# Selective scan in a ViT tower: seven of 32 B rows reach GpSimd by broadcast transfer of fp32 rows

## The reference, cut to what matters

```python
sel = jnp.einsum('ble,se->bls', xc, sel_w)
dt_in = sel[..., :R_]
Bm = sel[..., R_:R_ + N_]
Cm = sel[..., R_ + N_:]
dt = jax.nn.softplus(jnp.einsum('blr,er->ble', dt_in, dt_w) + dt_b)
dA = jnp.exp(dt[..., None] * A)
dBu = dt[..., None] * Bm[:, :, None, :] * xc[..., None]
def step(h, inp):
    dA_t, dBu_t, C_t = inp
    h = dA_t * h + dBu_t
    y = jnp.einsum('ben,bn->be', h, C_t)
    return (h, y)
```

## Time and profile before

| | before |
|---|---|
| median of 3 runs | 1512.79 us |
| lowest, highest | 1504.69, 1515.6 us |
| the profiled execution | 1513.76 us, span 1512.0 us |
| PE busy | 1292.1 us (85%) |
| DVE busy | 1031.3 us (68%) |
| ACT busy | 592.0 us (39%) |
| POOL busy | 455.7 us (30%) |
| mean granted clock of PE | 0.943 of full |

### The profile page before, as it was taken

How to read it: one execution, slowest core, us unless ns; L and a number is a source line. 1 busy time by engine, 2 the same in 40 slices (tenths; PEclk the granted TensorE clock), 3 DMA queues, 4 the chain that set the end, 5 groups by cost and what they waited for, 6 DMA issues and landing times. The chain is left out here.

```text
span 1512.0 us, 16650 instructions
## 1 busy us (share of the span) xinstructions
PE 1292.1 (85%) x5930; PEld 562.1 (37%) x5930; DVE 1031.3 (68%) x1130; ACT 592.0 (39%) x815; POOL 455.7 (30%) x230
## 2 busy tenths in 40 slices
PE   6957789989995778998998677999899677899988
PEld 2222333348532223333742223333473232333366
DVE  3599965664449996567555999556756599865683
ACT  0354343333425344332525443532451634343245
POOL 3268800022005881001200788000210189600030
PEclk9979999997897999999999799999999889999998
DMA  8334420000003342000001344200000134220000
GB/s 245 104 129 155 146 69 12 1 1 1 15 0 129 143 143 83 22 1 1 2 15 44 113 149 143 69 2 1 1 1 15 59 125 167 98 57 0 1 2 15
DMA packets 43379, 93.66 MB, mean 62 GB/s; under 512 B 6786, under 2 KB 23970, under 8 KB 42786
## 3 DMA queue, kind: packets, MB, share of 16 engines
q1 hardware_dynamic: 42690, 88.25, 17.5%
q10 hardware_dynamic: 608, 4.34, 1.0%
HBM read 87.84 MB, written 4.73 MB: 61 GB/s over the span
## 5 line engine op out<-in xcount | busy, mean ns | idle before, releaser
L448 POOL TENSOR_TENSOR scratch<-scratch 128x1024 f32<-128x1024 f32 x124 | 297.4, 2413 | 354.7 <-DVE scratch L1152 353.1
L598 PE MATMUL ps<-scratch,consts 128*128 128x512 f32 x512 | 257.8, 638 | 6.2 <-POOL scratch L448 6.2
L462 POOL TENSOR_TENSOR scratch<-scratch,rmax 128x1024 f32<-128x1024 f32 x32 | 61.6, 1925 | 598.3 <-DVE rmax L1272 598.3
L1152 DVE TENSOR_TENSOR_SCAN scratch<-ps,scratch 128x1024 f32<-128x1024 f32 x100 | 225.5, 2278 | 0.5
L925 ACT ACTIVATE ps<-steps,vec 128x1024 f32<-128x1024 f32 x128 | 142.9, 1117 | 207.1 <-DVE scratch L1152 205.2
L1201 DVE TENSOR_TENSOR scratch<-scratch,ps 128x1024 f32<-128x1024 f32 x108 | 131.8, 1221 | 128.6 <-PE ps L659 117.7
L576 PE MATMUL ps<-bc,pick 128*128 128x512 bf16 x256 | 84.7, 416 | 139.0 <-DVE scratch L1141 101.7
L971 ACT ACTIVATE scratch<-ps 128x1024 f32<-128x1024 f32 x108 | 108.9, 1023 | 175.5 <-PE ps L646 175.5
L598 PEld LDWEIGHTS ps<-scratch,consts 128*128 128x128 f32 x512 | 104.8, 207 | 127.2 <-issue 100.5
L646 PE MATMUL ps<-h_odd,w 64*128 64x512 f32 x512 | 140.9, 636 | 3.8 <-ACT scratch L971 3.8
L1141 DVE TENSOR_TENSOR scratch<-steps,ps 128x1024 f32<-128x1024 f32 x100 | 122.0, 1220 | 28.8 <-PE ps L576 23.5
(11 more groups left out here) (197 smaller groups left out, 1610.0 us busy)
## 6 DMA issues: line engine op xcount, KB each, us to landing
scratch<-c_rows SPq DMA_DIRECT2D x128, 512.0 KB, 3.7
steps<-routed_table SPq DMA_DIRECT2D x128, 64.5 KB, 1.9
decayT<-in_decayT SPq DMA_DIRECT2D x8, 512.0 KB, 15.6
work<-in_table ACTq DMA_DIRECT2D x1, 2064.0 KB, 13.2
routed_table<-work SPq DMA_DIRECT2D x1, 2064.0 KB, 6.3
w<-in_w ACTq DMA_DIRECT2D x4, 512.0 KB, 20.8
out<-h_even SPq DMA_DIRECT2D x4, 512.0 KB, 2.6
bc<-in_x_next SPq DMA_DIRECT2D x3, 512.0 KB, 3.6
```

The lines of the kernel that those rows point to most:

```text
L448: pool.tensor_tensor(hc_slot(k), hs_slot(k), c_slot(k), ALU.mult).then_inc(sem["hc_ready"], 1)
L598: m = mm(ps[:, 6 + c, :], ident, hc_slot(k)[:, c * CH:(c + 1) * CH], start=(n == 0), stop=(n == NS - 1))
L1152: dve.tensor_tensor_scan(hs_slot(k), banks(dA_bank(k)), dbu_slot(k), 0.0, ALU.mult, ALU.add).then_inc(sem["scanned"], 1)
```

## The change

For the seven POOL units B[n] no longer goes through PE and ACT. The store to DRAM now takes all 32 rows (B and C) of each batch instead of the 16 C rows, from the same fp32 tiles; SP loads row B[n] with a broadcast into `b_sb`, like a C row. SP's new transfer for unit j stands in front of the C load of unit j-1 and waits for the scan of the POOL unit before (j-4). POOL's multiply for j stands behind hc of unit j-3, one place later than before, and waits for the transfer. PE spreads B for the 25 DVE units only, in their own order, and ACT's copies are gone.

```diff
-B_ORDER = list(range(2 * NS))
-for _j in POOL_DRIVES:
-    B_ORDER[_j - 1:_j + 1] = [_j, _j - 1]
+DVE_DRIVES = [k for k in range(2 * NS) if k not in POOL_DRIVES]
@@ block.sync, move
-                sp.dma_start(c_dram[0], c_rows(0)[NS:2 * NS]).then_inc(sem["c_stored"], 16)
+                sp.dma_start(c_dram[0], c_rows(0)).then_inc(sem["c_stored"], 16)
...
-                        sp.dma_start(c_dram[1], c_rows(1)[NS:2 * NS]).then_inc(sem["c_stored"], 16)
+                        sp.dma_start(c_dram[1], c_rows(1)).then_inc(sem["c_stored"], 16)
                     if k == NS:
                         sp.wait_ge(sem["c_stored"], at(pair, "c_stored", 32))
+                    if k + 1 in POOL_DRIVES:
+
+                        n_ = POOL_DRIVES.index(k + 1)
+                        if n_:
+                            sp.wait_ge(sem["scanned"], at(pair, "scanned", POOL_DRIVES[n_ - 1] + 1))
+                        g_, row = divmod(k + 1, NS)
+                        sp.dma_start(b_sb, c_dram[g_, row].partition_broadcast(P)).then_inc(sem["b_loaded"], 16)
                     if k >= C_RING:
                         sp.wait_ge(sem["hc_ready"], at(pair, "hc_ready", k - C_RING + 1))
-                    sp.dma_start(c_slot(k), c_dram[g, n].partition_broadcast(P))\
+                    sp.dma_start(c_slot(k), c_dram[g, NS + n].partition_broadcast(P))\
@@ block.gpsimd
-                    if k + 4 in POOL_DRIVES:
-                        j = k + 4
+                    if k + 3 in POOL_DRIVES:
+                        j = k + 3
...
-                        pool.wait_ge(sem["b_copied"], at(pair, "b_copied", n_))
+                        pool.wait_ge(sem["b_loaded"], at(pair, "b_loaded", 16 * n_))
@@ block.tensor, spread_b and the loop that calls it
-                    k = B_ORDER[i]
+
+                    k = DVE_DRIVES[i]
...
                     if i:
-                        last = B_ORDER[i - 1]
-                        if last in POOL_DRIVES:
-                            pe.wait_ge(sem["b_copied"], at(pair, "b_copied", POOL_DRIVES.index(last) + 1))
-                        else:
-                            pe.wait_ge(sem["dbu_ready"], at(pair, "dbu_ready", drives_up_to(last)))
+                        pe.wait_ge(sem["dbu_ready"], at(pair, "dbu_ready", i))
...
-                    if k + 2 in POOL_DRIVES:
-                        spread_b(k + 1)
-                        spread_b(k + 2)
-                    elif k and k + 1 < 2 * NS and k + 1 not in POOL_DRIVES:
-                        spread_b(k + 1)
+                    if k in DVE_DRIVES[1:-1]:
+                        spread_b(DVE_DRIVES.index(k) + 1)
@@ block.scalar
-                def copy_b(j):
-                    act.wait_ge(sem["b_ps"], at(pair, "b_ps", B_ORDER.index(j) + 1))
...
-                    act.activation(b_sb, banks(0), ACT.Copy).then_inc(sem["b_copied"], 1)
...
-                    if k + 2 in POOL_DRIVES:
-                        copy_b(k + 2)
@@ block.vector, drive
-                    dve.wait_ge(sem["b_ps"], at(pair, "b_ps", B_ORDER.index(k) + 1))
+                    dve.wait_ge(sem["b_ps"], at(pair, "b_ps", drives_up_to(k)))
```

More of the change, by code:

```diff
@@ L70 @@
     dt_read=2, dt_exp=2, dt_ln=2, dt_ready=1, dt_late=NN, mid_late=1, u_ready=1, u_late=NN,
-    b_ps=2 * NS, dA_ready=2 * NS, dbu_ready=2 * NS - len(POOL_DRIVES), b_copied=len(POOL_DRIVES),
+    b_ps=2 * NS - len(POOL_DRIVES), dA_ready=2 * NS, dbu_ready=2 * NS - len(POOL_DRIVES), b_loaded=16 * len(POOL_DRIVES),
     dbu_pool=len(POOL_DRIVES), scanned=2 * NS, hc_ready=2 * NS - 1, hc_last=NC,
@@ L145, in build_tower @@
         fiT = sb("fiT", [P, 2, HID])
-        c_dram = nc.dram_tensor("c_rows", (2, NS, T), F32, kind="Internal").ap()
+        c_dram = nc.dram_tensor("bc_rows", (2, 2 * NS, T), F32, kind="Internal").ap()
         table_dram = nc.dram_tensor("routed_table", (P, LAYERS, NX, WCOL), F32, kind="Internal").ap()
@@ L926, in decay @@
                        .then_inc(sem["dA_ready"], 1)
-                def copy_b(j):
-                    act.wait_ge(sem["b_ps"], at(pair, "b_ps", B_ORDER.index(j) + 1))
-                    n_ = POOL_DRIVES.index(j)
-                    if n_:
-                        act.wait_ge(sem["scanned"], at(pair, "scanned", POOL_DRIVES[n_ - 1] + 1))
-                    else:
-                        act.wait_ge(sem["c_stored"], at(pair, "c_stored", 16))
-                    act.activation(b_sb, banks(0), ACT.Copy).then_inc(sem["b_copied"], 1)
                 first_parts(0)
```

## The result

| | before | after |
|---|---|---|
| median of 20 runs | 1520.07 us | 1497.95 us |
| lowest, highest | 1504.68, 1727.38 us | 1488.3, 1518.05 us |
| the profiled execution's span | 1512.0 us | 1493.3 us |
| four stretches of scans, added | 459.28 us | 444.19 us |

The ratio is 0.9883 with an interval of 0.9848 to 0.9917: 1.17% faster, where 0.78% was forecast. In pair 1 of the kernel before these are the two DVE rows

A forecast was written before the change was run, and what follows sets the result against it. DVE sets the pace in the scans, POOL next. Removed waits of 4.26 us a pair (17.0 in all), less 1.3 for held pieces, leave 2.94, or 11.8 in four pairs: 1512.79 to 1501.0 us, range 1488 to 1516.

The forecast's parts named there:

- the prediction's own signs: Expected in the trace: spread waits about 5 us, four units 12.75, stated piece lengths, no POOL wait for B.
- Spreads and copies removed: PE and ACT: busy time buys nothing; DVE's shorter waits for spreads give 4.26 us a pair, 17.0 in all.
- POOL's drive one place later: POOL's drive starts after hc j-3, ending at 8.3 for scan j at about 10.45; costs nothing by itself.
- The 2.1 us of slack: Time POOL's drive has in hand before scan j needs it, said to cover the later place.
- The pieces: DVE's small two-tile instructions, held by running POOL multiplies: 1.3 us given back of 4.26 a pair.
- The walk: Step through DVE's eight pieces in a pair against POOL's multiplies, ending 2.94 us ahead.
- The mis-sized term: DVE's piece L1178 after scan 24, held by hc 23: 1.98 us, not 1.40, so 0.58 lost a pair.
- rival A: Pieces after scans 4, 7, 8 and 24 not held by POOL: 1487.6 us, with half of it 1495; chance 0.18.
- the 4.5 of the sum: B load's assumed landing in us, between middle 3.7 and worst 6.0 of the C loads.
- Rival B: More pieces held, or PE's sums become the wait, 2 to 4 us a pair back: say 1511 us; chance 0.17.
- Rival C: B load lands late, past 8.0 us, delaying POOL's drive: 1549 us at 10; chance 0.09 with its second way.
- the second way of rival C: Fewer spreads halve PE's clock in a pair's last sums and projections: 36 us, 1537; chance 0.09 with late load.

The follow-up runs named there:

- e8: Changed kernel with the seven spreads that follow a POOL unit made twice, without the chain: scans 448.97 us, ratio 0.9894 to the kernel before.
- e3: Kernel before with only POOL's drive moved behind hc of unit j-3, spreads and copies kept: scans 456.13 us, ratio 0.9913.
- e7: Changed kernel with SP sending B's load one scan later, after scan j-3: scans 459.65 us, ratio 1.0071 to the kernel before.
- e2: Changed kernel without B's loads, POOL multiplying by tile xc instead (wrong output): scans 447.48 us, ratio 0.9816 to the kernel before.
- e6: Changed kernel with POOL's drive put back behind hc of unit j-4, transfer kept: scans 486.23 us, ratio 1.0156 to the kernel before.
- e5: Changed kernel with DVE's pieces at other scans, two bc pieces made one, gating behind the last products: scans 429.71 us, ratio 0.9823.
- e4: Changed kernel with only the tables changed, moving DVE's pieces to other scans: scans 436.31 us, ratio 0.9721 to the kernel before.
- e1: Changed kernel with PE spreading all 32 rows and ACT copying seven into an unread tile again: scans 456.01 us, ratio 1.0013.
- e9: e5 with B's load in front of the C load of unit j-2 instead of j-1: scans 425.68 us, ratio 0.9767 to the kernel before.

## Why the prediction was right

Forecast 1501.0 us, 0.78% under the median of before; measured 1.17% (0.83 to 1.52), so the mechanism and the side were right and the size somewhat low. In the profile: 11.8 us forecast from the scans, 15.1 and 12.6 measured in two profiles. What the first has over the forecast comes by luck from one piece, as told below. By the prediction's own signs two things did not come as said: POOL was not to wait for B, and waited 12 times, and the piece after scan 24 had another length.

- **Spreads and copies removed.** Right. The waits for the spread fell to 5.8 us where about 5 was said, and the busy time on PE and ACT bought nothing (e8).
- **POOL's drive one place later.** Right in the sum: the piece after scan 6 fell to 0.40, 2.05 us a pair, of which the pieces after scans 7 and 8 take some 1.4 back (e3: 1.57 and 0.93 instead of 0.69 and 0.40); what is left, about 0.7 a pair, is most of what the place alone gives (e3, 3.2 us in four pairs). The 2.1 us of slack were there for DVE: POOL waits up to 1.3 us for B without a scan waiting for POOL. e7, later by a whole scan, is past it.
- **The pieces.** The walk gave about 1.7 to 1.9, 0.40, 1.7 to 1.9 for the first three and measured were 1.71, 0.40 and 1.72; the fourth, which it had end 0.37 ahead, took 0.93 and ended 0.58 ahead, counted from the first scan. In pair 2, where the gating piece took 1.99 as forecast, the stretch is 2.78 us shorter than before, with 2.94 forecast. The trace agrees with the Trainium skill ("SBUF — State Buffer", the section on the two physically separate sides) that whoever starts first keeps the other out, on both sides: the piece is held (1.99), or hc is (pair 1).
- **The mis-sized term: the gating after scan 24.** I gave it 1.98 in each pair, 0.58 lost. Measured were 0.67, 1.99, 1.04 and 0.67, so that instead of 2.3 us lost 1.2 were won: these 3.5 us are the whole of the 3.3 by which the forecast was too small. In the second profile (7.2 in sum) 1.6 were lost, and the scans came within 0.8 us of the forecast. Behind this term stands the sentence that POOL should not wait for the loads. I had B's load go out at the end of scan j-4, since the C load in front of it on the queue waited for an older hc. For unit 25 that is hc 20, and it was not yet done: scan 21 ended at 159.68, but hc 20 was the second of three from 155.91 and ended near 160.6, and the queue shows B's issue just behind it (SP), 1.3 us late:

```profile
158.29 2.63 SPq L371 DMA_DIRECT2D scratch<-bc_rows  x2
160.98 0.42 SPq L368 DMA_DIRECT2D work<-bc_rows  x1
```

  This load landed after 5.36 us, at 166.3, and POOL's drive started 0.86 us late, as much as the lead that the walk gives POOL at this place: 9.14 - 8.3 = 0.84, not the "0.9 us or more" that the text on rival A says. In the four pairs the load of unit 25 went out 1.3, 1.1, 1.5 and 1.9 us after scan 21 and landed 5.4, 5.0, 5.7 and 4.9 us later. The landing was in the range of 4 to 6, though over the 4.5 of the sum; alone it would have made POOL wait at this unit in no pair, since B was wanted at 5.95. An engine's lag behind the scans, which I had not put into the queue's wait, came on top. e2, without the load, is the kernel of my walk, and has 1.96 or 1.97 in every pair.
- **Rival A, the pieces get in freely:** false for the three early pieces, true for the gating piece in two pairs of the first profile and in none of the second (0.90 at the least), and by the cause that the rival names, B's landing. **Rival B, the gain is used up:** false, two drives wait for 0.5 us and no further piece was caught. (Its price was added up wrongly: 2 to 4 us in each of four pairs give 1509 to 1517, not 1505 to 1515.) **Rival C, the load comes late:** false here, but its mechanism is real and near: one scan later (e7) or one place earlier (e6) brings it, and e6 costs 42 us more than the change in the scans. PE's clock was 1.00 in the last 10 us of the pair's scans, so the second way of rival C did not come either.

## What to carry to other kernels

When an engine sets the pace without waiting for anything, look for instructions of one shape with two lengths: here the same piece takes 0.40 or 2.45 us, and moving the pieces to scans for which the other engine itself waits, or into a wait, gave about as much in the scans (444 to 430 us, e5) as the change itself. Work such a table out again from the trace after each change, because removed waits shift which places are free (e4). And a transfer that shares a queue goes when the one in front of it may go: before counting its landing time, work out what that one waits for, with the lag of the engine that releases it.

## What was unexpected of the hardware

**PE at half clock while fully busy.** The stretch between two pairs' scans lasts 253 to 259 us, but in some pairs of several kernels 267 to 269: in the kernel before once, in e1 twice, in e3, e7 and e9 once (and in e9 once more behind the last pair), in the changed kernel not in its two profiles. It is a place in the attention block; here pair 1 of the kernel before (columns as in the earlier trace rows; the clock is the third number from the end):

```profile
340.00:350.00 10.00, 10.00 (x62) 7.54 (x62) 5.29 (x11) 2.25 (x3) 1.90 (x1) 0.50 0.01 2
350.00:360.00 10.00, 10.00 (x63) 8.54 (x62) 5.31 (x8) 3.09 (x4) 2.05 (x2) 0.52 0.00 0
```

and pair 2 of the same execution, at the same place of the program:

```profile
720.00:730.00 10.00, 10.00 (x114) 8.15 (x114) 8.82 (x17) 5.05 (x7) 4.00 (x3) 1.00 0.01 2
730.00:740.00 10.00, 10.00 (x110) 8.90 (x108) 6.82 (x14) 5.94 (x9) 3.81 (x2) 1.00 0.01 2
```

```profile
325.60:335.60 10.00, 5.94 (x56) 3.16 (x49) 9.75 (x12) 3.03 (x3) 4.63 (x3) 1.00 0.00 0
707.70:717.70 10.00, 5.94 (x56) 3.16 (x49) 9.75 (x12) 3.03 (x3) 4.63 (x3) 1.00 0.01 2
```

So the program's work in these 10 us does not decide it. One such stretch costs 11 to 13 us, nearly as much as the change is worth. That e1 and e3, equal in their scans to 0.1 us, have ratios 1.0% apart may come from it; only one execution of each has a trace, so this is not shown. What decides it stays open.

**The hold is not quite to the end.** A held piece is let go 0.11 to 0.15 us before POOL's recorded end, in all held pieces of these runs, if the piece then takes its usual time. And POOL is held in the same way: an hc that finds a piece running begins in the records but ends later by what is left of it, less about as much: hc 23 takes 2.89 us instead of 2.35 beside a piece of 0.67.
